# Router products issued among the row-tile transposes in three feed-forward stages

## The chip, the cores and the metric

The kernel runs on one core of a Trainium2 chip. The metric is the device time of one execution in microseconds (us); lower is better. The engines are named as in the profile: PE is TensorE's matmul side, PEld its weight loads, DVE is VectorE, ACT is ScalarE, POOL is GpSimd, SP is SyncE, which only starts DMAs here.

## The reference, cut to what matters

The program is a four-layer network over 2048 tokens (2 x 1024) of width 256. Each layer adds a gated cross-attention and then a gated mixture-of-experts feed-forward to `x`. The feed-forwards of layers 0, 1 and 3 choose experts per token from a linear router; what the change touches is that router's first step:

```python
# layer 0: x here is the layer-normalised input, 2048 x 256, Wr is 256 x 8
router_logits = x @ Wr
router_probs = softmax(router_logits, axis=-1)
expert_idx = argmax(router_probs, axis=-1)
...
# layer 1: Wg is 256 x 8, two experts per token
gating = softmax(X @ Wg + bg, axis=-1)
...
# layer 3: wg is 32 x 256, four experts per token out of four of eight groups
logits = xf @ wg.T
scores = softmax(logits, axis=-1)
```

Everything behind it (which expert, which row of the expert's buffer, the experts' own products, the sum back into `x`) depends on these logits. All arithmetic is float32.

## The kernel before, in words

Tokens lie in SBUF as 16 row tiles of 128 tokens (`TILES = 16`), each 256 wide, so a tile has two 128-column chunks (`DC = 2`). The kernel is written engine by engine: each stage is a block in which every engine has its own list of instructions in program order, and the engines meet through semaphores. No scheduler reorders anything; a stage ends in a barrier of all engines.

A feed-forward stage (`l0_ffn`, `l1_ffn`, `l3_ffn`) begins alike in all three layers. DVE computes the layer-norm statistics (`row_statistics`), then normalises tile after tile (`normalize_dve`, L115; in layer 3 the loop at L2830) and counts `staged` up. PE turns each normalised tile: two transposes per tile into one of four PSUM banks (`turn_pe`, L126; in layer 3 the same loop written out at L2730). ACT copies each turned tile from PSUM to `chip.xt` in SBUF (`turn_act`, L136) and counts `turned_read`; PE waits for that count before it reuses a bank. These two transposes of a tile are called T below.

When all 16 tiles have been turned, PE multiplies them by the router's weights (L604, L832, L2736): per tile two matmuls, one per chunk, with the turned tile as stationary operand and 8 columns of weights (32 in layer 3) as the moving one. These are called R. A float32 matmul runs as two passes, each with its own weight load, so R has two matmuls per tile in the program and four in the trace, 64 for the stage; T has two in both, 32 for the stage. One weight load with its matmul is called a pair: a stage has 96 of them.

The last R counts `routed`. DVE waits for it, then walks a chain of small operations (softmax, choice, ranks with two more matmuls by `rank_pe`, slots) up to `placed`. POOL waits for `placed` and scatters the rows to the experts' buffers in DRAM with indirect DMAs; SP waits for the scatters and loads the first expert's rows; PE waits for those. While all this goes on, SP's queue clears the buffers and loads the first experts' weights.

The lines of the transposes' loop and of R in layer 0 before:

```python
turn_pe(pe, chip, turn, p_hidden)
pe.wait_ge(loaded, 16)
for t in range(TILES):
    pe.wait_ge(turn.turned_read, t + 1)
    for c in range(DC):
        ins = pe.matmul(p_route[:, t * E:(t + 1) * E], chip.xt[:, c, t * P:(t + 1) * P], wr[:, c, :], ...)
ins.then_inc(routed, 1)
```

`turn_pe` is also called in the attentions of layers 1 and 3 and in the feed-forward of layer 2; those calls have no R with them in the changed kernel either.

Of the kernel before, what the change touches and what calls it, by code (L numbers as in the profile page):

```python
# [115 lines left out]
                          ALU.subtract, ALU.mult).then_inc(s.staged, 1)  # L116


def turn_pe(pe, chip, s, psum):

    for t in range(TILES):
        pe.wait_ge(s.staged, t + 1)
        if t >= TURN_BANKS:
            pe.wait_ge(s.turned_read, t + 1 - TURN_BANKS)
        for c in range(DC):
            ins = pe.transpose(psum[:, t % TURN_BANKS, c * P:(c + 1) * P], chip.xn[:, t, c * P:(c + 1) * P], chip.ident[:])  # L126
        ins.then_inc(s.turned, 1)


def turn_act(act, chip, s, psum, scale=None, bias=None):  # L130
# [374 lines left out]
def l0_ffn(nc, chip, I):  # L505
# [10 lines left out]
    with ExitStack() as stack:  # L516
# [78 lines left out]
        @block.tensor  # L595
        def _(pe):
            pe.wait_ge(b_loaded, 16)
            pe.transpose(p_y[:, 0:E * FC], b1_rows[:], chip.ident[0:E * FC, 0:E * FC]).then_inc(b1_turned, 1)
            turn_pe(pe, chip, turn, p_hidden)
            pe.wait_ge(loaded, 16)  # L600
            for t in range(TILES):
                pe.wait_ge(turn.turned_read, t + 1)
                for c in range(DC):
                    ins = pe.matmul(p_route[:, t * E:(t + 1) * E], chip.xt[:, c, t * P:(t + 1) * P], wr[:, c, :],  # L604
                                    start=c == 0, stop=c == DC - 1)
            ins.then_inc(routed, 1)
            pe.wait_ge(chose, 1)
            rank_pe(pe, chip, chosen[:], p_route[:, 128:256].rearrange("p (e t) -> p e t", e=E),
                    p_route[:, 256:384].rearrange("p (e t) -> p e t", e=E)).then_inc(ranked, 1)
            pe.wait_ge(placed, 1)  # L610
            pe.sem_inc(h_done, FC)
            pe.sem_inc(y_done, 1)

            def turn_rows(loads):
                pe.wait_ge(x_loaded, loads)
                for c in range(DC):
                    ins = pe.transpose(p_xt[:, c * P:(c + 1) * P], x_tile[:, c * P:(c + 1) * P], chip.ident[:])
                ins.then_inc(x_turned, 1)

            turn_rows(16)  # L620
            g = one_register(pe, "l0f_pe_g")
            with pe.Fori(0, E // 2) as i:
                for u in range(2):
                    pe.wait_ge(w_loaded[u], i * 32 + 32)
                    pe.sem_inc(passed, 1)
                    with tiles_of_expert(pe, tile_counts, i * 2 + u, g, MAX_TILES) as at:
                        pe.wait_ge(x_kept, at)
                        for f in range(FC):
                            for c in range(DC):
                                ins = pe.matmul(p_hidden[:, f // CB, (f % CB) * P:(f % CB + 1) * P], w1[:, u, c, f * P:(f + 1) * P], xt_tile[:, c * P:(c + 1) * P],  # L630
                                                start=c == 0, stop=c == DC - 1)
                            ins.then_inc(h_done, 1)
                        turn_rows(at * 16 + 16)
                        pe.wait_ge(y_kept, at)
                        for f in range(FC):
                            pe.wait_ge(h_kept, at * FC + (f + 1))
                            ins = pe.matmul(p_y[:, 0:D], hidden[:, f, :], w2[:, u, f, :], start=f == 0, stop=f == FC - 1)
                        ins.then_inc(y_done, 1)
# [80 lines left out]
def l1_ffn(nc, chip, I):  # L719
# [7 lines left out]
    with ExitStack() as stack:  # L727
# [95 lines left out]
        @block.tensor  # L823
        def _(pe):
            pe.wait_ge(b_loaded, 32)
            pe.transpose(p_y[:, 0:2 * E * FC], b13_rows[:], chip.ident[0:2 * E * FC, 0:2 * E * FC]).then_inc(b_turned, 1)
            turn_pe(pe, chip, turn, p_h)
            pe.wait_ge(loaded, 32)
            for t in range(TILES):
                pe.wait_ge(turn.turned_read, t + 1)  # L830
                for c in range(DC):
                    ins = pe.matmul(p_route[:, t * E:(t + 1) * E], chip.xt[:, c, t * P:(t + 1) * P], wg[:, c, :],  # L832
                                    start=c == 0, stop=c == DC - 1)
            ins.then_inc(routed, 1)
            pe.wait_ge(chose, 1)
            rank_pe(pe, chip, chosen[:], p_route[:, 128:256].rearrange("p (e t) -> p e t", e=E),
                    p_route[:, 256:384].rearrange("p (e t) -> p e t", e=E)).then_inc(ranked, 1)
            pe.wait_ge(placed, 1)
            pe.sem_inc(h_done, 4)
            pe.sem_inc(y_done, 1)  # L840

            def turn_rows(loads):
                pe.wait_ge(x_loaded, loads)
                for c in range(DC):
                    ins = pe.transpose(p_xt[:, c * P:(c + 1) * P], x_tile[:, c * P:(c + 1) * P], chip.ident[:])
                ins.then_inc(x_turned, 1)

            turn_rows(16)
            g = one_register(pe, "l1f_pe_g")
            with pe.Fori(0, E // 2) as i:  # L850
                for u in range(2):
                    pe.wait_ge(w_loaded[u], i * 48 + 48)
                    pe.sem_inc(passed, 1)
                    with tiles_of_expert(pe, tile_counts, i * 2 + u, g, MAX_TILES) as at:
                        pe.wait_ge(x_kept, at)
                        pe.wait_ge(h3_kept, at * 4)
                        pe.wait_ge(h13_kept, at * 4)
                        for half in range(2):
                            for bank, w in ((2 + half, w3), (half, w1)):
                                for f in (2 * half, 2 * half + 1):  # L860
                                    for c in range(DC):
                                        ins = pe.matmul(p_h[:, bank, (f % 2) * P:(f % 2 + 1) * P], w[:, u, c, f * P:(f + 1) * P],  # L862
                                                        xt_tile[:, c * P:(c + 1) * P], start=c == 0, stop=c == DC - 1)
                                ins.then_inc(h_done, 1)
                        turn_rows(at * 16 + 16)
                        pe.wait_ge(y_kept, at)
                        for f in range(FC):
                            pe.wait_ge(h_kept, at * 3 + max(f, 1))
                            ins = pe.matmul(p_y[:, 0:D], hidden[:, f, :], w2[:, u, f, :], start=f == 0, stop=f == FC - 1)
                        ins.then_inc(y_done, 1)  # L870

            pe.wait_ge(b2_loaded, 48)
            for t in range(TILES):
                s = t % 4
                if t >= 2:
                    pe.wait_ge(mixed_kept, t - 1)
                pe.wait_ge(mix_steps, 2 * t + 2)
                for c in range(DC):
                    ins = pe.transpose(p_h[:, t % 2, c * P:(c + 1) * P], mixed[:, s, c * P:(c + 1) * P], chip.ident[:])
                ins.then_inc(mixed_turned, 1)  # L880
                pe.wait_ge(mixed_kept, t + 1)
                if t >= 2:
                    pe.wait_ge(added, t - 1)
                for c in range(DC):
                    pe.matmul(p_h[:, 2 + t % 2, 0:D], mixed_t[:, s, c * P:(c + 1) * P], wf[:, c, :], start=c == 0, stop=False)
                pe.matmul(p_h[:, 2 + t % 2, 0:D], chip.ones[0:1, :], bf[:], start=False, stop=True).then_inc(out_done, 1)
# [1688 lines left out]
def l3_ffn(nc, chip, I, out):  # L2575
# [14 lines left out]
    with ExitStack() as stack:  # L2590
# [129 lines left out]
        def _(pe):  # L2720
# [1 line left out]
            for c in range(DC):  # L2722
                ins = pe.transpose(p_y[:, 0, c * E:(c + 1) * E], wg_rows[:, c * P:(c + 1) * P], chip.ident[0:E, 0:E])
            ins.then_inc(wg_turned, 1)
            for t in range(TILES):
                pe.wait_ge(turn.staged, t + 1)
                if t >= TURN_BANKS:
                    pe.wait_ge(turn.turned_read, t + 1 - TURN_BANKS)
                for c in range(DC):
                    ins = pe.transpose(p_h[:, t % TURN_BANKS, c * P:(c + 1) * P], x_ext[:, t, c * P:(c + 1) * P], chip.ident[:])  # L2730
                ins.then_inc(turn.turned, 1)
            pe.wait_ge(wg_kept, 1)
            for t in range(TILES):
                pe.wait_ge(turn.turned_read, t + 1)
                for c in range(DC):
                    ins = pe.matmul(p_y[:, 1, t * E:(t + 1) * E], chip.xt[:, c, t * P:(t + 1) * P], wg[:, c, :],  # L2736
                                    start=c == 0, stop=c == DC - 1)
            ins.then_inc(routed, 1)

# [222 lines left out]
```

## Time and profile before

| | us |
|---|---|
| median of 3 runs | 3436.51 |
| lowest and highest run | 3435.71, 3441.28 |
| span of the profiled execution (first to last instruction) | 3429.7 |
| busy in the span: PE, PEld, DVE, ACT, POOL | 2900.1, 2111.7, 1886.9, 1407.8, 608.0 |
| mean granted TensorE clock over the span | 0.902 |

The profiled execution is known by its span; it is 6.8 us shorter than the median of the runs, which are timed from outside. A time in the trace is counted from the span's start. The granted clock is given as a share of 2.4 GHz: 1.00 is 2.4 GHz, 0.50 is 1.2 GHz, and it has no level between; a value between belongs to a stretch in which it changed. A busy share over the whole span says little here, since the program is a row of stages with different limits: the stretches of the three feed-forward beginnings are near 106, 794 and 2973 us.

### The profile page before, as it was taken

The page shows a single profiled execution, that of the slowest core. Times are in us where ns is not written, and L with a number is a line of the kernel's source. Part 1 is how long each engine was busy: PE and PEld are TensorE (multiplying, and loading weights), DVE is VectorE, ACT ScalarE, POOL GpSimd, SP SyncE. Part 2 cuts the span into 40 slices and gives each one's busy share as a digit, 9 for nine tenths or more (in the row PEclk, how much of TensorE's full clock was granted, in tenths as well). Part 3 has the DMA queues.
Part 4 walks back from the last instruction along what each step waited for, and adds up shares of the span by engine and source line. Part 5 has one row for each costly group of instructions (what it writes and reads, how often), then busy time and mean ns, then how long its engine had stood idle before and what let it go on. Part 6 is the DMA issues. An engine that isn't in the chain of part 4 may idle for free. (4 is left out here: it accounts for less than half of the span.)

```text
span 3429.7 us, 46832 instructions
## 1 busy us (share of the span) xinstructions
PE 2900.1 (85%) x13932; PEld 2111.7 (62%) x13933; DVE 1886.9 (55%) x3558; ACT 1407.8 (41%) x2923; POOL 608.0 (18%) x571
## 2 busy tenths in 40 slices
PE   6495879972898798999789999999999998355997
PEld 5495545532786487999556666666666665233664
DVE  4312555403454336444478888888888886352332
ACT  1141544420221114444447777776777776100110
POOL 0202111113102120000201111111111111144554
PEclk7698889985998598999889999999999999577998
DMA  1443010005222101000010001000011000425775
GB/s 37 168 144 96 1 27 14 14 1 217 84 99 77 35 1 50 25 24 0 10 28 21 22 14 35 14 21 20 15 25 24 22 14 2 168 81 152 173 172 134
DMA packets 158692, 195.46 MB, mean 57 GB/s; under 512 B 39057, under 2 KB 129320, under 8 KB 154952
## 3 DMA queue, kind: packets, MB, share of 16 engines
q1 hardware_dynamic: 122072, 131.88, 12.8%
q0 software_dynamic: 22192, 40.13, 4.9%
q10 hardware_dynamic: 14304, 22.02, 1.9%
q8 instruction: 50, 0.82, 0.1%
q14 instruction: 74, 0.61, 0.1%
HBM read 105.38 MB, written 67.80 MB: 50 GB/s over the span
## 5 line engine op out<-in xcount | busy, mean ns | idle before, releaser
L1849 ACT ACTIVATE l3a_pt_hi<-l3a_banks 128x512 fp32r<-128x512 f32 (+2 forms) x640 | 382.0, 597 | 316.7 <-PE l3a_banks L1795 253.8
L1956 DVE TENSOR_TENSOR l3a_pt_lo<-l3a_pt,l3a_pt_hi 128x512 fp32r<-128x512 f32 (+2 forms) x640 | 460.3, 724 | 90.5 <-ACT l3a_pt L1850 85.9
L1850 ACT ACTIVATE l3a_pt<-l3a_banks 128x512 f32<-128x512 f32 (+2 forms) x640 | 378.0, 591 | 0.0
L1930 DVE TENSOR_REDUCE l3a_maxima<-l3a_banks 128x1 f32<-128x1178 f32 x256 | 351.4, 1376 | 2.4 <-PE l3a_banks L1746 1.1
L1795 PE MATMUL l3a_banks<-l3a_pt_hi,l3a_v 128*65 128x512 f32 (+2 forms) x640 | 286.3, 447 | 7.7 <-ACT l3a_out L1864 7.7
L1805 PE MATMUL l3a_banks<-l3a_q,l3a_k 128*128 128x512 f32 (+2 forms) x640 | 256.8, 401 | 7.2 <-ACT l3a_pt L1850 3.3
L1806 PE MATMUL l3a_banks<-l3a_q,l3a_k 72*128 72x512 f32 (+5 forms) x640 | 253.6, 396 | 0.0
L1795 PE MATMUL l3a_banks<-l3a_pt_hi,l3a_v_lo 128*65 128x512 f32 (+2 forms) x640 | 252.6, 395 | 0.0
L1795 PE MATMUL l3a_banks<-l3a_pt_lo,l3a_v 128*65 128x512 f32 (+2 forms) x640 | 252.4, 394 | 0.0
L1746 PE MATMUL l3a_banks<-l3a_k,l3a_q 128*128 128x512 f32 (+1 forms) x768 | 216.2, 392 | 15.4 <-DVE l3a_maxima L1930 14.3
L1746 PEld LDWEIGHTS l3a_banks<-l3a_k,l3a_q 128*128 128x128 f32 x768 | 141.8, 195 | 61.6 <-DVE l3a_maxima L1930 39.3
L2713 POOL DMA_INDIRECT l3f_sums<-l3f_y_rows,l3f_token_index x96 | 145.7, 1518 | 155.4 <-DVE l3f_row_weight L2905 130.7
L1984 POOL PARTITION_BROADCAST l3a_shared<-l3a_inverse x65 | 63.3, 975 | 618.2 <-issue 618.2
L1988 POOL TENSOR_TENSOR l3a_out_t<-l3a_out,l3a_shared 64x512 f32<-64x512 f32 x65 | 88.2, 1356 | 473.7 <-issue 473.7
L1805 PEld LDWEIGHTS l3a_banks<-l3a_q,l3a_k 128*128 128x128 f32 (+2 forms) x640 | 115.8, 181 | 78.1 <-ACT l3a_pt L1850 9.9
L1795 PE MATMUL l1a_banks<-l1a_pt,l1a_v 128*65 128x512 f32 (+2 forms) x320 | 153.3, 602 | 1.7 <-ACT l1a_out L1864 1.7
L1437 ACT ACTIVATE l2f_hidden_hi<-l2f_p_h,l2f_b_pair 128x512 fp32r<-128x512 f32 x128 | 89.2, 697 | 151.3 <-PE l2f_p_h L1390 140.1
L2821 ACT ACTIVATE l3f_silu<-l3f_p_h 128x320 f32<-128x320 f32 x64 | 28.0, 437 | 295.7 <-PE l3f_p_h L2783 295.7
L1489 DVE TENSOR_TENSOR l2f_hidden_lo<-l2f_hidden,l2f_hidden_hi 128x512 fp32r<-128x512 f32 x128 | 88.6, 692 | 107.6 <-ACT l2f_hidden L1438 107.6
L862 PE MATMUL l1f_p_h<-l1f_xt_tile,l1f_w 128*128 128x128 f32 x1184 | 141.5, 278 | 7.1 <-issue 6.1
L862 PEld LDWEIGHTS l1f_p_h<-l1f_xt_tile,l1f_w 128*128 128x128 f32 x1184 | 136.8, 194 | 14.9 <-issue 14.8
L2783 PE MATMUL l3f_p_h<-l3f_xt,l3f_w 128*128 128x320 f32 x512 | 144.5, 436 | 1.1 <-DVE l3f_xt L2895 1.1
(524 smaller groups left out, 6053.1 us busy)
## 6 DMA issues: line engine op xcount, KB each, us to landing
l3f_w<-in_L_ffn_w SPq DMA_DIRECT2D x96, 256.0 KB, 3.2
l0f_w<-in_L_ffn_W ACTq DMA_DIRECT2D x12, 1024.0 KB, 6.6
l3f_slots_x<-l3f_empty SPq DMA_DIRECT2D x10, 1168.0 KB, 14.3
l3f_x_rows<-l3f_slots_x SPq DMA_DIRECT2D x32, 292.0 KB, 3.9
l1f_w<-in_L_ffn_W ACTq DMA_DIRECT2D x18, 512.0 KB, 4.6
l2f_w<-in_L_ffn_w SPq DMA_DIRECT2D x16, 512.0 KB, 4.7
l3a_q<-l3a_q SPq DMA_DIRECT2D x64, 128.0 KB, 2.3
l3a_k<-l3a_k SPq DMA_DIRECT2D x64, 128.0 KB, 2.3
```

The lines of the kernel that those rows point to most:

```text
L862: ins = pe.matmul(p_h[:, bank, (f % 2) * P:(f % 2 + 1) * P], w[:, u, c, f * P:(f + 1) * P], xt_tile[:, c * P:(c + 1) * P], start=c == 0, s ...
L1437: act.activation(hidden_hi[:, n % 2, f, :], p_h[:, f, :], ACT.Gelu, bias=bias)
L1746: ins = pe.matmul(banks[:, c, 0:end - at], lhs, a.k1[:, u, h, at:end], start=True, stop=not masked)
L1795: ins = pe.matmul(a.o_bank[0:HEAD + 1, :], v[0:rows, u, c, h, :], pt[0:rows, slot, :], start=c == 0 and k == 0, stop=c == KEY_CHUNKS - 1 a ...
L1805: pe.matmul(a.st_bank[0:rows, n % 2, :], a.k1[:, u, h, row:row + rows], a.q1[:, u, h, queries], start=True, stop=False)
L1806: pe.matmul(a.st_bank[0:rows, n % 2, :], a.k2[second, u, h, row:row + rows], a.q2[second, u, h, queries], start=False, stop=True).then_inc ...
L1849: act.activation(a.pt_hi[0:rows, n % a.pt_slots, :], a.st_bank[0:rows, n % 2, :], ACT.Exp, bias=bias, scale=scale)
L1850: act.activation(a.pt[0:rows, n % 4, :], a.st_bank[0:rows, n % 2, :], ACT.Exp, bias=bias, scale=scale).then_inc(a.exped, 1)
L1930: dve.tensor_reduce(a.maxima[:, n:n + 1], banks.rearrange("p a b -> p (a b)")[:, 0:KEYS], AX.X, ALU.max).then_inc(a.maxed, 1)
L1956: dve.tensor_tensor(a.pt_lo[0:rows, slot, :], a.pt[0:rows, n % 4, :], a.pt_hi[0:rows, slot, :].bitcast(F32), ALU.subtract).then_inc(a.lo_m ...
L2713: pool.indirect_dma_start(sums, bass.IndirectOffsetOnAxis(token_index[0:n, u, j:j + 1], 0), y_rows[0:n, u, j, :], None, compute_op=ALU.add ...
L2783: ins = pe.matmul(p_h[:, k + f, 0:CAP], w[:, u, c, f * P:(f + 1) * P], xt[:, u, c, :], start=c == 0, stop=c == DC - 1)
```

## The change

In the three stages PE no longer does all T and then all R. `turn_pe` takes a `route` function and calls it for tile t - 2 right behind the transposes of tile t; the last two tiles' R follow behind the last transposes. Each R waits for ACT's copy of its own tile, as before. The waits for the router's weights (`loaded` in layers 0 and 1, `wg_kept` in layer 3) now stand ahead of the first transpose. Layer 3 calls `turn_pe` instead of its own copy of the loop. Nothing is added or taken away from the arithmetic, the buffers or the DMAs.

```diff
+ROUTE_LAG = 2
...
+def turn_pe(pe, chip, s, psum, source=None, route=None):
...
+    source = chip.xn if source is None else source
     for t in range(TILES):
         pe.wait_ge(s.staged, t + 1)
         if t >= TURN_BANKS:
             pe.wait_ge(s.turned_read, t + 1 - TURN_BANKS)
         for c in range(DC):
-            ins = pe.transpose(psum[:, t % TURN_BANKS, c * P:(c + 1) * P], chip.xn[:, t, c * P:(c + 1) * P], chip.ident[:])
+            ins = pe.transpose(psum[:, t % TURN_BANKS, c * P:(c + 1) * P], source[:, t, c * P:(c + 1) * P], chip.ident[:])
         ins.then_inc(s.turned, 1)
+        if route is not None and t >= ROUTE_LAG:
+            pe.wait_ge(s.turned_read, t - ROUTE_LAG + 1)
+            route(t - ROUTE_LAG)
+    if route is None:
+        return None
+    for t in range(TILES - ROUTE_LAG, TILES):
+        pe.wait_ge(s.turned_read, t + 1)
+        ins = route(t)
+    return ins
...
-            turn_pe(pe, chip, turn, p_hidden)
             pe.wait_ge(loaded, 16)
-            for t in range(TILES):
-                pe.wait_ge(turn.turned_read, t + 1)
+
+            def route(t):
                 for c in range(DC):
                     ins = pe.matmul(p_route[:, t * E:(t + 1) * E], chip.xt[:, c, t * P:(t + 1) * P], wr[:, c, :],
                                     start=c == 0, stop=c == DC - 1)
-            ins.then_inc(routed, 1)
+                return ins
+
+            turn_pe(pe, chip, turn, p_hidden, route=route).then_inc(routed, 1)
```

The edit of layer 1 reads the same with its own names; in layer 3 the loop of transposes goes and `turn_pe(pe, chip, turn, p_h, x_ext, route)` stands for it.

PE's list in the feed-forward of layer 0, from the bias transpose to the rank matmuls, before (`l0f_p_hidden<-chip_ident` is T, `l0f_p_route<-l0f_wr` is R, one row of the list stands for the program's matmuls, not for their passes):

```order
L598 MATMUL l0f_p_y<-chip_ident,l0f_b_rows 128x64
L126 MATMUL l0f_p_hidden<-chip_ident,chip_xn 128x128 x32
L604 MATMUL l0f_p_route<-l0f_wr,chip_xt 128x8 x32
L441 MATMUL l0f_p_route<-l0f_chosen,chip_before 128x128
L442 MATMUL l0f_p_route<-l0f_chosen,chip_ones 128x128
```

The beginning of the same list in the changed kernel:

```order
L612 MATMUL l0f_p_y<-chip_ident,l0f_b_rows 128x64
L131 MATMUL l0f_p_hidden<-chip_ident,chip_xn 128x128 x6
L617 MATMUL l0f_p_route<-l0f_wr,chip_xt 128x8 x2
L131 MATMUL l0f_p_hidden<-chip_ident,chip_xn 128x128 x2
L617 MATMUL l0f_p_route<-l0f_wr,chip_xt 128x8 x2
L131 MATMUL l0f_p_hidden<-chip_ident,chip_xn 128x128 x2
L617 MATMUL l0f_p_route<-l0f_wr,chip_xt 128x8 x2
```

The 32 transposes in a row have become six, and then two at a time with the two matmuls of an earlier tile behind them.

The end of the list in layer 3, changed (`l3f_p_h<-chip_ident` is T, `l3f_p_y<-l3f_wg` is R):

```order
L131 MATMUL l3f_p_h<-chip_ident,l3f_x_ext 128x128 x2
L2745 MATMUL l3f_p_y<-l3f_wg,chip_xt 128x32 x2
L131 MATMUL l3f_p_h<-chip_ident,l3f_x_ext 128x128 x2
L2745 MATMUL l3f_p_y<-l3f_wg,chip_xt 128x32 x6
L2773 MATMUL l3f_p_y<-l3f_chosen,chip_before 128x512
L2774 MATMUL l3f_p_y<-l3f_chosen,chip_ones 128x512
```

Behind the last transposes six matmuls of R are left, those of three tiles, where 32 stood before.

## Rows read from the trace of the kernel before

**Rows 1.** The page's first line.
```profile
span 3429.7 us, 46832 instructions
```
**Rows 2.** Waits: who waited for whom, us in total, times, longest.
```profile
POOL l0f_slots_x L582 <- DVEq L694: 31.0, 1, 31.0
PE l0f_p_xt L617 <- DMA l0f_x_tile<-l0f_slots_x: 28.0, 1, 28.0
...
POOL l1f_slots_x L809 <- DVEq L950: 36.1, 1, 36.1
...
POOL l3f_slots_x L2704 <- DVEq L2880: 8.9, 1, 8.9
```
**Rows 3.** Timeline, layer 0: start, us, engine, line, tiles, count, idle before it.
```profile
96.42 0.37 SPq L553 DMA_DIRECT2D l0f_wr<-in_L_ffn_Wr  x1
...
105.68 5.26 DVE L115 TENSOR_SCALAR chip_xn<-chip_x,chip_mean,chip_inv_std 128x256 f32<-128x256 f32 x16
...
106.15 6.06 PE L126 MATMUL l0f_p_hidden<-chip_ident,chip_xn 128*128 128x128 f32 x32 [6.87 <-DVE chip_xn L115]
...
106.88 5.89 ACT L136 COPY chip_xt<-l0f_p_hidden 128x256 f32<-128x256 f32 x16 [15.42 <-PE l0f_p_hidden L126]
...
112.05 8.65 PE L604 MATMUL l0f_p_route<-l0f_wr,chip_xt 128*128 128x8 f32 x64
...
120.74 0.29 DVE L678 TENSOR_REDUCE l0f_best<-l0f_p_route 128x16 f32<-128x128 f32 x1 [9.66 <-PE l0f_p_route L604]
```
**Rows 4.** Timeline, layers 1 and 3, the same places.
```profile
794.02 5.45 PE L126 MATMUL l1f_p_h<-chip_ident,chip_xn 128*128 128x128 f32 x32 [6.02 <-DVE chip_xn L115]
...
809.07 0.29 DVE L930 TENSOR_TENSOR l1f_logits<-l1f_p_route,l1f_bg 128x128 f32<-128x128 f32 x1 [10.12 <-PE l1f_p_route L832]
...
2972.88 0.22 DVE L2828 COPY l3f_wg<-l3f_p_y 128x64 f32<-128x64 f32 x1
...
2973.48 6.04 PE L2730 MATMUL l3f_p_h<-chip_ident,l3f_x_ext 128*128 128x128 f32 x32 [6.81 <-DVE l3f_x_ext L2830]
...
2988.20 0.69 DVE L2835 TENSOR_REDUCE l3f_best<-l3f_p_y 128x16 f32<-128x512 f32 x1 [9.91 <-PE l3f_p_y L2736]
```
**Rows 5.** Stretches: from:to, length, PE busy (count), granted clock, DMA share, GB/s.
```profile
106.15:110.71 4.56, 4.56 (x22) 0.50 1.01 408
110.71:112.05 1.34, 1.34 (x13) 1.00 1.02 422
112.05:117.54 5.49, 5.49 (x52) 1.00 0.99 337
117.54:120.70 3.16, 3.16 (x16) 0.50 1.08 374
794.02:796.79 2.77, 2.77 (x13) 0.50 1.01 417
...
803.62:809.03 5.41, 5.41 (x26) 0.50 1.00 409
2973.48:2977.91 4.43, 4.43 (x21) 0.50 1.01 422
...
2984.74:2988.16 3.42, 3.42 (x17) 0.50 1.01 420
```
**Rows 6.** One line's instructions in short stretches: count, ns min/median/max, first and last start.
```profile
L126 PE MATMUL l0f_p_hidden<-chip_ident,chip_xn x17: 421/421/421, 106.6 to 110.0; 128*128 128x128 f32 x17
...
L604 PE MATMUL l0f_p_route<-l0f_wr,chip_xt x39: 256/256/256, 112.8 to 117.0; 128*128 128x8 f32 x39
...
L604 PE MATMUL l0f_p_route<-l0f_wr,chip_xt x13: 361/361/362, 117.8 to 120.3; 128*128 128x8 f32 x13
...
L2736 PE MATMUL l3f_p_y<-l3f_wg,chip_xt x15: 401/401/402, 2984.8 to 2987.8; 128*128 128x32 f32 x15
```
**Rows 7.** Layer 3's attention, its 32 transposes by the same helper: line's starts, stretch.
```profile
L126 PE MATMUL l3a_banks<-chip_ident,chip_xn x32: 417/421/474, 1699.7 to 1709.3; 128*128 128x128 f32 x32
...
1699.70:1709.35 9.65, 9.24 (x32) 0.50 0.00 0
```

More of the change, by code:

```diff
@@ L116, in normalize_dve @@
                           ALU.subtract, ALU.mult).then_inc(s.staged, 1)
-def turn_pe(pe, chip, s, psum):
+ROUTE_LAG = 2
+def turn_pe(pe, chip, s, psum, source=None, route=None):
+    source = chip.xn if source is None else source
     for t in range(TILES):
@@ L826, in _, with route @@
             pe.transpose(p_y[:, 0:2 * E * FC], b13_rows[:], chip.ident[0:2 * E * FC, 0:2 * E * FC]).then_inc(b_turned, 1)
-            turn_pe(pe, chip, turn, p_h)
             pe.wait_ge(loaded, 32)
-            for t in range(TILES):
-                pe.wait_ge(turn.turned_read, t + 1)
+            def route(t):
                 for c in range(DC):
@@ L833, in _ @@
                                     start=c == 0, stop=c == DC - 1)
-            ins.then_inc(routed, 1)
+                return ins
+            turn_pe(pe, chip, turn, p_h, route=route).then_inc(routed, 1)
             pe.wait_ge(chose, 1)
@@ L2724, in _, with route @@
             ins.then_inc(wg_turned, 1)
[L2725 to L2731, printed above, removed]
             pe.wait_ge(wg_kept, 1)
-            for t in range(TILES):
-                pe.wait_ge(turn.turned_read, t + 1)
+            def route(t):
                 for c in range(DC):
@@ L2737, in _ @@
                                     start=c == 0, stop=c == DC - 1)
-            ins.then_inc(routed, 1)
+                return ins
+            turn_pe(pe, chip, turn, p_h, x_ext, route).then_inc(routed, 1)
             def shared_block(b):
```

## The prediction

> **What bounds the kernel now.** I first looked at where the three touched stretches stand in the chain of work, then at what PE does in them. The waits say that they are on the path in all three layers: POOL's scatter waits for DVE's routing chain for 31.0, 36.1 and 8.9 us, and PE's first expert waits 28.0 us for the scattered rows [rows 2]. At the head of that chain DVE waits for the last R: 9.66, 10.12 and 9.91 us of idle time stand before its first routing step [rows 3, 4]. So a microsecond more or less between the first transpose and that DVE step goes to the end of the kernel almost whole. I call that distance the stage's length. Before, it is 120.74 - 106.15 = 14.59 us in layer 0, 809.07 - 794.02 = 15.05 us in layer 1 and 2988.20 - 2973.48 = 14.72 us in layer 3 [rows 3, 4].
>
> Next, who is slow in these 14 to 15 us? PE. Cut where its granted clock changes, every stretch is busy from end to end: 4.56 of 4.56, 1.34 of 1.34, 5.49 of 5.49, 3.16 of 3.16 us [rows 5]. DVE normalises 16 tiles in 5.26 us, 0.33 us each, and ACT copies 16 in 5.89 us [rows 3], while PE at the low clock needs 2 x 0.213 = 0.427 us for a tile's two transposes (price below). There is no gap among the transposes into which R could slip. **Interleaving can therefore save nothing by filling PE's idle time; it only changes in which order PE does the same 96 pairs.** What is left to decide is at which clock it does them.
>
> The prices of a pair come from the starts of neighbouring matmuls [rows 6]. T at granted clock 0.50 (1.2 GHz): 17 starts from 106.6 to 110.0, 3.4 / 16 = 0.213 us. R at 0.50: 13 starts from 117.8 to 120.3, 2.5 / 12 = 0.21 us; layer 3's R with 32 columns, 15 starts in 3.0 us, the same 0.21. R at 1.00 (2.4 GHz): 39 starts from 112.8 to 117.0, 4.2 / 38 = 0.111 us. So T and R cost the same, 0.213 us at the low clock and 0.111 at the full one, whatever number of columns R moves. I use 0.2133 and 0.112 below, within what these roundings leave.
>
> Now the clock [rows 5]. In layer 0 it stands at 0.50 for the first 4.56 us of transposes, is 1.00 from 110.71 to 117.54, and falls to 0.50 for the last 3.16 us, in which 16 matmuls of R take what about 28 would take at 1.00. It rose while PE did nothing but transposes, and it fell after 5.49 us in which PE did nothing but R, without a pause. Layers 1 and 3 show the same: up after 2.77 and 4.43 us of transposes, down for the last 5.41 and 3.42 us of R. A dense row of transposes is what earned the clock in each of these stages, and R did not hold it, though PE counts as busy throughout.
>
> **The change part by part.** It takes away that dense row. After the first six transposes PE repeats four pairs of R and two of T: at 0.2133 us a pair, two transposes every 6 x 0.2133 = 1.28 us, 1.6 per us. In layer 0 before they came at 22 in 4.56 us, 4.8 per us [rows 5]. Between these the trace has one more case, the attention of layer 3: 32 transposes by the same helper in 9.65 us, 3.3 per us, and the clock stayed 0.50 to the end [rows 7]. The new stream has half that density of transposes, and R between them, which failed to hold the clock where it ran alone. I take it that **the clock stays at 0.50 through the whole stage**.
>
> Then a stage is 96 pairs at the low price: 95 x 0.2133 = 20.26 us from the first start to the last, plus the last matmul's 0.361 us (0.401 in layer 3) [rows 6] and 0.04 us until DVE starts: 20.67 us, 20.71 in layer 3. Against before:
>
> - layer 0: 20.67 - 14.59 = +6.1 us
> - layer 1: 20.67 - 15.05 = +5.6 us
> - layer 3: 20.71 - 14.72 = +6.0 us
>
> Sum +17.7 us. Seen another way, each stage loses some 6.83 us at full clock, 61 pairs at 0.112, which cost 0.101 more each: 61 x 0.101 = 6.2 us, less the little that transposes at full clock had lost to waiting for ACT.
>
> The other edits. The wait for the router's weights, moved ahead of the transposes, costs nothing: layer 0's `wr` was issued at 96.42, nearly 10 us before the first transpose [rows 3]; layer 3's copy of `wg` starts at 2972.88 and ends 0.4 us before the first transpose at 2973.48 [rows 4], and DVE does it ahead of the normalising that PE waits for anyway. If the weights came late, the price would be that lateness, once per stage; behind PE's wait then stand all transposes and ACT's copies. The new wait of R for ACT's copy two tiles back costs nothing either: from the first transpose's start at 106.15 to the first copy's start is 0.73 us, and a copy takes 5.89 / 16 = 0.37 us [rows 3], 1.10 us in all; between a tile's transposes and its R lie at least the six first transposes, 1.28 us, and later 14 pairs, 2.99 us. Queued behind that wait would be the next transposes, and behind them ACT. The four PSUM banks are now never the limit, as R's wait has already seen a later copy. No DMA, POOL or SP instruction moves; DVE and ACT have their old lists. Later work moves 6 us against its weight loads, which only come earlier relative to it. A later clock change can fall a little differently: I allow 3 us to either side over the rest of the kernel, about half the spread of the three runs (3435.71 to 3441.28).
>
> The sum stands against the profiled execution's span of 3429.7 us [rows 1], which would become 3447.4. The median of the runs is 6.8 us longer than the span; with it, 3436.5 + 17.7 = **3454.2 us**, with 3451 to 3458 as this case's own range.
>
> **The rivals.** *A: the mixed stream gets the full clock when the transposes did, and keeps it.* This is the case not slower. For it speaks that PE is just as busy as before from end to end, and that transposes recur in the stream, where before 5.49 us of R had none. Against it speak both facts above: the clock fell under uninterrupted R, and did not rise under 3.3 transposes per us [rows 5, 7]. The Trainium skill's page "TensorE: Matmul & The Clock Gate", section "Why this matters for your kernels", has it that an engine kept continuously busy with matmuls gets past the low clock; by that rule this rival would be the outcome. The trace agrees for transposes and disagrees for R, which was continuous and lost the clock. Price: 21.4 pairs in the first 4.56 us, then 74.6 at 0.112 = 8.4 us, and 0.3 at the end: 13.2 us in layer 0, -1.4; likewise 2.77 + 83 x 0.112 + 0.3 = 12.4 us in layer 1, -2.7, and 4.43 + 75.2 x 0.112 + 0.3 = 13.1 us in layer 3, -1.6. Sum -5.7 us, 3430.8. It decides where 1.6 transposes per us with R between them suffice. If the clock rises but falls again as before, there is nothing to win, 3436. Even the best of this is no gain over 0.2%, 6.9 us, which is about what a measurement of this kernel can tell from no change.
>
> *B: only layer 3 gets the clock*, since its R moves 32 columns where the others move 8. Against it: its R alone lost the clock like the others. Price: 6.1 + 5.6 - 1.6 = +10.1 us, 3446.6.
>
> *C: the lag of two tiles is too short and PE stands still before each R.* It decides if a tile's way through ACT takes over 2.99 us, where the rows give 1.10. If each of the 14 R among the transposes waited for one copy of 0.37 us, a stage would grow by 5.2 us more: 17.7 + 15.6 = +33.3, 3470. That the change does something else than it says is ruled out by PE's list in the changed kernel.
>
> **How the numbers follow.** The forecast has 0.78, A 0.12, B 0.06, C 0.04. Forecast, B and C are slower by over 0.2%: 0.88. Of A I give 0.09 to no difference and 0.03 to a gain over 0.2%, for the case that a later stage also gains some clock. The range reaches from B with its error down to 3444, and up to 3462, between the forecast's upper end and C; A and C stay outside, 0.16.
>
> **What would show it.** In the changed trace each of the three stages should show granted clock 0.50 from its first transpose to its last R, 361 ns as the duration of R's matmuls in layers 0 and 1 where 256 stood for those at full clock, and DVE's wait for R grown from about 10 us to 16. The mean granted clock should fall from 0.902 to about 0.897: 3 x 6.83 us less at full clock. Layer 2's feed-forward, which has the same helper and an unchanged order, should keep its length. The prediction is wrong if a stretch among the mixed pairs shows 1.00, if PE has gaps before R, or if the stage grows by 6 us and the scatter behind it does not start later.

## The result and the profile after

The changed kernel takes 3446.2 us, median of 12 runs (3440.5 to 3458.4), the kernel before 3437.65 us in the 12 runs beside it (3429.5 to 3443.1). The ratio is 1.0028 with a 95% interval of 1.0015 to 1.0041: the change makes the kernel slower by 9.6 us (0.28%), 5 to 14 us; the two medians differ by 8.6 us.

The first rows to read are the three stretches from the first transpose to DVE's first routing step, one line each for layers 0, 1 and 3 (from:to, length, PE busy and count, granted clock, DMA share, GB/s). Before:

```profile
106.15:120.74 14.59, 14.55 (x96) 0.73 1.02 376
794.02:809.07 15.05, 15.01 (x96) 0.73 1.01 415
2973.48:2988.20 14.72, 14.68 (x96) 0.73 1.01 423
```

After:

```profile
94.90:114.10 19.20, 19.13 (x96) 0.50 1.03 374
789.60:808.76 19.16, 19.12 (x96) 0.50 1.00 392
2981.60:3000.88 19.28, 19.17 (x96) 0.50 1.01 423
```

The same 96 matmuls, PE counted as busy from end to end in both; what differs is the granted clock. (A matmul's record is longer than the step to the next one, 0.36 us against 0.21 at the low clock, so a short wait can hide in a full busy time; where it matters below, the steps between starts are read instead.) The spell at 1.00 that each stage had [rows 5] is gone from all three, and they are 19.2 us long (19.16, 19.16 and 19.20 from the first transpose's own start; the windows above begin up to 0.08 us earlier). Against the stages of before that is +4.6, +4.1 and +4.5 us, 13.2 in the sum.

One line's instructions in layer 0, and who waited for it (us, times); R is L617 now:

```profile
L617 PE MATMUL l0f_p_route<-l0f_wr,chip_xt x64: 221/361/361, 96.2 to 113.7; 128*128 128x8 f32 x64
...
who waited for it (us, times):
  DVE l0f_best L693: 14.3, 1
```

R's median matmul is 361 ns, the duration that [rows 6] show at 0.50, and the stretch above has 0.50 throughout: nothing of R ran at 1.00 any more. (The 221 ns belong to the first R behind each pair of transposes, also at 0.50; more on it below.) DVE waits 14.3 us for it where it had waited 9.66 [rows 3].

The waits further down the chain, in layers 0 and 1:

```profile
POOL l0f_slots_x L596 <- DVEq L709: 35.6, 1, 35.6
...
POOL l1f_slots_x L824 <- DVEq L966: 40.3, 1, 40.3
```

They stood at 31.0 and 36.1 us [rows 2]: the scatter begins 4.6 and 4.2 us later relative to POOL's own start, as much as the stages have grown. In layer 3 POOL's wait for `placed` stayed at 8.9 us, because POOL has an earlier wait in the same chain, and that one grew, from 54.7 to 59.3 us. The first scatter of layer 3, before and after (timeline):

```profile
3034.88 1.23 POOL L2704 DMA_INDIRECT l3f_slots_x<-l3f_x_ext,l3f_scatter_index  x1 [8.87 <-DVEq L2880]
3047.58 1.23 POOL L2720 DMA_INDIRECT l3f_slots_x<-l3f_x_ext,l3f_scatter_index  x1 [8.88 <-DVEq L2891]
```

That is 46.7 us behind DVE's first routing step in both (2988.20 and 3000.88). In layers 0 and 1 the scatter begins 9.4 and 13.4 us behind that step in both kernels, and PE's first expert 33.2 and 57.4 us behind it (57.1 in layer 3), within 0.1 us. So up to the first expert none of the delay is made up in any of the three layers.

### The profile page after: what moved, and what is told of

It is laid out like the page before. It is cut to its first block and busy times, and to the rows that moved or that the text cites. A ratio compares the mean times of both kernels' runs of the same rounds, so it can differ in the third digit from the quotient of the medians.

```text
span 3446.4 us, 46832 instructions
## 1 busy us (share of the span) xinstructions
PE 2915.7 (85%) x13932; PEld 2126.6 (62%) x13933; DVE 1881.5 (55%) x3558; ACT 1411.1 (41%) x2923; POOL 611.5 (18%) x571
## 5 line engine op out<-in xcount | busy, mean ns | idle before, releaser
L878 PEld LDWEIGHTS l1f_p_h<-l1f_xt_tile,l1f_w 128*128 128x128 f32 x1184 | 137.6, 195 | 14.9 <-issue 14.7
```

## The experiments

Eight more kernels ran, and both kernels of the case once more, all on one chip. The theory under test is the prediction's: the stage is longer because the mixed stream does not get the full clock. Its rival is that mixing costs by itself, through waits for ACT's copies or through the changes between transposes (T) and router matmuls (R).

**Putting a denser row back.** In the first two only the lag differs from the changed kernel.

```diff
-ROUTE_LAG = 2
+ROUTE_LAG = 12
```

> The changed kernel with a lag of 12 tiles in place of 2: 26 transposes stand in a row before the first R; then three tiles mixed, then the rest of R. Clock theory (the stage is longer because no dense row of transposes earns the full clock): the clock rises to 1.00 among the dense transposes as it did before the change, for 6.8 us or longer, and a stage from first transpose to DVE's first routing step is 13.5 to 15.5 us, as before (14.6 to 15.1). Rival, the mixing itself costs (waits for ACT, switches between transposes and R): the three mixed tiles of 14 keep their share of the 4.4 us that the change cost, about 1 us more than before, 15.6 to 16 us, at whatever clock.

The three stages (same columns as above):

```profile
96.14:113.29 17.15, 17.11 (x96) 0.60 1.02 378
789.69:806.83 17.14, 17.10 (x96) 0.60 1.01 408
2975.99:2990.31 14.32, 14.28 (x96) 0.74 1.01 423
```

The clock came back in all three, but for 3.4 us in two of them and 6.8 us in the third (the mean clock's excess over 0.50, times twice the length): 17.1, 17.1 and 14.3 us. My expectation of 13.5 to 15.5 us missed two of three, because I took the length of the spell from a single execution. The rival's 15.6 to 16 us, the same in each stage, missed all three. Three stages with the same list differ by 2.8 us, so what sets the length is not the list alone; with a mean clock of 0.60 they are 17.1 us, with 0.74 14.3 us.

With a lag of 8:

> The same with a lag of 8 tiles: 18 transposes in a row (3.8 us at the low clock), then seven mixed tiles, then R. Clock theory: stage by stage one of two lengths, nothing between them in proportion to the mixing: where the dense row earns the clock 13 to 15 us, with a stretch at 1.00; where it does not, 19 to 20 us, all at 0.50. Rival, the mixing costs: half of the 4.4 us in every stage, 17 us, without regard to the clock.

```profile
104.03:123.84 19.81, 19.77 (x96) 0.50 1.02 372
801.42:815.09 13.67, 13.63 (x96) 0.75 1.01 415
2980.79:2992.64 11.85, 11.81 (x96) 0.88 1.01 424
```

Nearly one list of instructions, apart from layer 3's 32 columns, and three lengths between 11.85 and 19.81 us, in the order of the clock. That is the clear case against the rival: half the mixing does not cost half, it costs what the clock makes of it. My own expectation allowed two lengths, 13 to 15 or 19 to 20 us; the 11.85 us lie outside, as there the clock, once up after 2.9 us, stayed up to the end, through seven mixed tiles and the R behind them. The single times of the two kernels, 3434.9 and 3436.9 us, say little beside a kernel before that runs from 3430 to 3446 us in the 23 runs of this set.

**Giving the clock before the stage begins.** PE is idle while DVE computes the norms, so it was given 28 transposes of the identity into a PSUM tile that nothing uses yet.

```diff
+WARM = 28
...
+def warm_pe(pe, chip, out):
...
+    for _ in range(WARM):
+        pe.transpose(out, chip.ident[:], chip.ident[:])
...
+            warm_pe(pe, chip, p_xt[:, 0:P])
             turn_pe(pe, chip, turn, p_hidden, route=route).then_inc(routed, 1)
```

With the order of before (lag 16):

> The order of before (lag 16: all transposes, then all R), and PE does 28 transposes of the identity into an unused PSUM tile just before each of the three stages, while DVE still computes the norms and PE would be idle. Clock theory: the first real transpose finds 1.00; DVE's 0.33 us per tile then sets the pace of the transposes (5.3 us), R begins at 0.112 us a pair and falls to 0.50 somewhere in its 64: a stage of 12.5 to 14 us, 1 to 2 us less than before, 3 to 6 us in the sum, about 3433 where before gives 3437. Rival, the clock does not matter for the length: 14.6 to 15.1 us as before.

Its stages were 15.0, 14.9 and 15.6 us, and the ratio to the kernel before 0.9987 (0.9976 to 0.9998). So the first transpose did find 1.00, but the stages gained nothing in this profile (45.5 us in the sum; the two profiles of the kernel before have 44.4 and 46.9), against what I expected. Layer 0, cut at the fall:

```profile
99.44:108.75 9.31, 9.31 (x71) 1.00 1.00 367
108.75:114.45 5.70, 5.66 (x28) 0.50 1.05 386
```

The full clock was spent on the transposes, which DVE paces at 0.33 us a tile when PE is fast, and was lost again in R: 28 of its matmuls ran at the low price. Whether the small gain in the total comes from these stages is left open.

With the changed order (lag 2):

> The changed order (lag 2) with the same 28 transposes of the identity ahead of each stage. Clock theory: the stage begins at 1.00 and stays there for 3.4 us at least; where the mixed stream holds the clock it takes 10.5 to 11.5 us, where it loses it 13 to 16 us, in either case several us under the 19.2 us of the changed kernel; the sum over the stages falls by 10 to 25 us against the changed kernel. Rival, the mixing itself costs (waits for ACT, switches): a stage stays at 19 us or near it, since PE would wait as before.

Layer 0 up to the fall and behind it, then layer 1 whole, then layer 3 up to the fall and behind it:

```profile
105.36:107.91 2.55, 2.55 (x22) 1.00 1.00 392
107.91:122.82 14.91, 14.87 (x76) 0.50 1.02 373
800.38:810.86 10.48, 10.44 (x96) 1.00 1.02 417
2979.97:2981.93 1.96, 1.96 (x16) 1.00 1.03 428
2981.93:2997.95 16.02, 15.98 (x82) 0.50 1.01 426
```

In layer 1 the clock happened to hold, and the 96 matmuls of the mixed stream went through in 10.48 us, 0.109 us each, with every wait for ACT and every change between T and R in it. So neither waits nor changes cost anything of note. In layers 0 and 3 the stream began at 1.00 and lost it after 2.55 and 1.96 us, where I had expected at least 3.4, and the stages took 17.5 and 18.0 us: one stage came out at the low end of my expectation, and the other two were 1.5 to 2 us longer than it allowed. The total has a ratio of 0.9983 (0.9969 to 0.9998). Why layer 1 held the clock and the others did not is not settled.

**Making R hold the clock.** The cleanest test leaves the number of matmuls, the weight loads and the order alone and changes only what R moves: 128 columns, the router's 8 (or 32) repeated by a stride of zero. (In layer 3 the last three tiles move 96, 64 and 32.) The surplus columns are overwritten later or never read.

```diff
-                    ins = pe.matmul(p_route[:, t * E:(t + 1) * E], chip.xt[:, c, t * P:(t + 1) * P], wr[:, c, :],
-                                    start=c == 0, stop=c == DC - 1)
+                    ins = pe.matmul(p_route[:, t * E:t * E + P].rearrange("p (r e) -> p r e", e=E), chip.xt[:, c, t * P:(t + 1) * P],
+                                    wr[:, c, :].unsqueeze(1).to_broadcast([P, P // E, E]), start=c == 0, stop=c == DC - 1)
```

With the changed order, without the warm-up:

> The changed order (lag 2), but each matmul of R moves 128 columns in place of 8 (layer 3: 32): the router's 8 columns repeated by a stride of zero, the surplus results overwritten by the next tile's. A pair at the full clock should cost 0.109 to 0.112 us as before, since a pair of a transpose, which also moves 128 columns, costs that. Clock theory: the mixed stream now earns the clock as the row of transposes did, after 2.8 to 5 us, and keeps it to the end: a stage of 12 to 13.5 us in all three layers, against 19.2 in the changed kernel; total 3431 to 3435 against 3439.9 of before. Rival, mixing itself costs or the clock follows the share of time in which PE is busy (which does not change): 19 to 20.5 us at 0.50, total as the changed kernel.

Each stage up to the rise of the clock and from there to its end, layers 0, 1 and 3:

```profile
104.50:110.12 5.62, 5.62 (x27) 0.50 0.99 399
110.12:118.07 7.95, 7.91 (x71) 1.00 1.02 350
793.42:796.19 2.77, 2.77 (x13) 0.50 1.00 414
796.19:805.63 9.44, 9.40 (x85) 1.00 1.01 413
2975.79:2980.73 4.94, 4.94 (x24) 0.50 1.01 423
2980.73:2988.95 8.22, 8.18 (x74) 1.00 1.01 421
```

The order is the changed kernel's to the instruction, PE is busy from end to end as there, and R does sixteen times (layer 3: up to four times) the arithmetic; yet the clock rises within 2.8 to 5.6 us, does not fall again, and the stages take 13.6, 12.2 and 13.2 us instead of 19.2. The total is 3430.2 us, ratio to the kernel before 0.9970 (0.9955 to 0.9984).

With the order of before and the same R:

> The order of before (all transposes, then all R) with R moving 128 columns. Clock theory: the clock rises as before and does not fall during R: a stage of 12 to 13.5 us, the same as with the mixed order, since PE is busy throughout in both. Rival, the order decides: clearly different from the mixed order with the same R. If the fall of the clock before had another cause than the few columns R moves, it falls again after 6.8 us and the stage takes 14.5 to 15 us.

```profile
106.97:120.13 13.16, 13.12 (x96) 0.84 1.00 375
794.98:808.66 13.68, 13.64 (x96) 0.79 1.01 416
2977.60:2990.67 13.07, 13.03 (x96) 0.84 1.02 427
```

13.1 to 13.7 us, as with the mixed order: at nearly equal clocks the order hardly matters where PE is the limit. And the fall of the clock in the kernel before was due to R's few columns: with 128 of them it did not fall in any of the three stages, where it fell in all six of the two profiles with few. The kernel's time is a single run, 3437.6 us, and says nothing beside the spread.

Both together, warm-up and wide R, with the changed order:

> The changed order, R moving 128 columns, and 28 transposes of the identity ahead of each stage. Clock theory: 1.00 from the first transpose to the last R in all three stages, 96 pairs at 0.109 to 0.112: 10.4 to 11 us each, 12 to 13 us less than before in the sum; total about 3427, and under both kernels. Rival, the clock at the start is luck and the stream loses it as it did twice with the narrow R: stages of 17 to 18 us.

and with the order of before:

> The same with the order of before. Clock theory: 1.00 throughout, but now DVE's 0.33 us a tile paces the transposes (5.3 us) and PE idles among them; then 64 pairs of R at 0.112, 7.2 us: 12.4 to 12.8 us a stage. So at a full clock the mixed order should be worth 2 us a stage, 6 us in all, which it could not show at the low clock. Rival, mixing is worth nothing at any clock: the same length as the mixed order within 0.3 us.

Stages of the mixed order, then of the order of before, each for layers 0, 1 and 3:

```profile
106.86:118.05 11.19, 11.15 (x96) 1.00 1.00 376
795.02:806.21 11.19, 11.15 (x96) 1.00 1.02 417
2970.01:2981.09 11.08, 11.04 (x96) 1.00 1.01 422
```

```profile
102.33:114.80 12.47, 12.43 (x96) 1.00 1.01 376
789.95:802.42 12.47, 12.43 (x96) 1.00 1.02 415
2970.07:2982.37 12.30, 12.26 (x96) 1.00 1.00 419
```

1.00 throughout in all six. Here the mixed order is worth 1.2 to 1.3 us a stage (I had expected 2), because at the full clock PE waits for DVE among the transposes when they stand alone, and R can fill that. The busy time does not show this wait; the starts do. Layer 1 with the order of before:

```profile
789.95 5.29 PE L138 MATMUL l1f_p_h<-chip_ident,chip_xn 128*128 128x128 f32 x32 [1.13 <-DVE chip_xn L115]
795.08 7.31 PE L854 MATMUL l1f_p_route<-l1f_wg,chip_xt 128*128 128x128 f32 x64
```

The 32 transposes take 5.13 us up to the first R, 0.16 us each, which is DVE's 0.33 us a tile. The mixed kernel takes 3423.8 us, ratio to the kernel before 0.9961 (0.9943 to 0.9979), 13 us less than before and better than both kernels; the other has 3431.2 us and 0.9980 (0.9968 to 0.9992). A stage is a little over my 10.4 to 11 us: 0.117 us a matmul, where the one stage at full clock with the narrow R had 0.109. The two transposes of one mixed tile and of the next, narrow and then wide, both in layer 1:

```profile
806.70 0.41 PE L138 MATMUL l1f_p_h<-chip_ident,chip_xn 128*128 128x128 f32 x2
807.31 0.41 PE L138 MATMUL l1f_p_h<-chip_ident,chip_xn 128*128 128x128 f32 x2
801.13 0.38 PE L138 MATMUL l1f_p_h<-chip_ident,chip_xn 128*128 128x128 f32 x2
801.79 0.38 PE L138 MATMUL l1f_p_h<-chip_ident,chip_xn 128*128 128x128 f32 x2
```

A tile takes 0.61 us with the narrow R and 0.66 with the wide one, which is six pairs at 0.11; 14 mixed tiles make this 0.7 us, the whole difference of the two stages. A row of wide R by itself (layer 1 above) costs (7.31 - 0.27) / 63 = 0.112 us a matmul, the narrow one 0.111 [rows 6].

**How much is chance.** Both kernels of the case were profiled once more.

> The kernel before, profiled once more, to see how much a stage's length differs between executions. Clock theory: each stage has one spell at 1.00 that begins among the transposes and ends in R; where it is 6.8 us long the stage is 13.5 to 15.2 us, where it is shorter correspondingly longer, about 0.9 us for each us at 1.00. Rival, the stage's length is fixed by its instructions: 14.6, 15.0 and 14.7 us again within 0.2.

Layer 0 in three parts, then layers 1 and 3 whole:

```profile
103.82:109.53 5.71, 5.71 (x27) 0.50 1.00 406
109.53:112.94 3.41, 3.41 (x33) 1.00 1.02 326
112.94:121.26 8.32, 8.28 (x40) 0.50 1.03 381
795.75:810.65 14.90, 14.86 (x96) 0.73 1.02 418
2978.55:2993.09 14.54, 14.50 (x96) 0.73 1.01 425
```

Layer 0's spell at 1.00 was 3.41 us this time and the stage 17.44 us, where the first profile had 6.83 and 14.59. The sum of the three stages is 46.9 us here and 44.4 there.

> The changed kernel, profiled once more. Clock theory: no spell at 1.00 in the three stages, and so no spread: 19.1 to 19.3 us each. Rival, the missing spell was chance: at least one of the stages has one and is shorter by a us or more.

```profile
105.51:124.67 19.16, 19.13 (x96) 0.50 1.02 374
799.92:819.09 19.17, 19.13 (x96) 0.50 1.00 393
2984.22:3003.42 19.20, 19.16 (x96) 0.50 1.01 425
```

The changed kernel repeats to 0.02 us: no spell, no spread. Of the 24 stages profiled with the narrow R, in all orders, 21 follow one rule: no time at 1.00 gives 19.2 to 19.8 us, 2 to 3.4 us give 17.1 to 18.0, 6.8 us give 13.7 to 15.05, 9 us give 11.9 (lag 8, layer 3), 10.5 us give 10.5. Only the three of the warmed order of before stand outside (8.5 to 9.5 us at 1.00, 14.9 to 15.6 us), since its transposes spend the full clock waiting for DVE. What sets the length of a spell, and whether one comes at a lag of 8, stays open. The single times of these two kernels are 3435.7 and 3449.5 us.

## Why the prediction was right, and which terms were off

**What bounds the stage: right.** PE is busy for 19.13 of 19.20 us after the change; there was no idle time to fill, and at the low clock the mixed order saves only the 1.5 us a stage that are worked out below.

**The path to the end: right as far as the first expert.** DVE's wait for R grew by what the stage grew in layer 0 (9.66 to 14.3 us), and scatter and first expert kept their distance from DVE's step in all three layers. Behind that, single executions differ by several us in stretches that the change does not touch: from DVE's step in layer 1 to the first transpose of layer 3 it is 2164 and 2168 us in the two profiles of before, 2173 and 2165 in the two of the changed kernel.

**The clock: right, and shown by more than the profile of the change.** The prediction took from [rows 5, 7] that the dense row of transposes earned the clock and that R did not hold it. The changed kernel has 0.50 in six of six stages. With R widened to 128 columns and nothing else changed, the clock came and stayed, with the transposes as thinly spread as in the changed kernel. So a dense row of transposes was one way to the clock and not the only one: going from 8 to 128 columns in R alone brought it back. Rival A, the mixed stream gets the full clock, is therefore out for the changed kernel; with R at 128 columns a mixed stream kept it in six of six stages. The rule weighed there, from the Trainium skill's page "TensorE: Matmul & The Clock Gate", section "Why this matters for your kernels", that keeping the engine continuously busy gets it past the low clock, does not fit here: PE was busy for 19.1 us on end at 0.50, and with the same order and a wider R it was at 1.00 after 2.8 to 5.6 us. The measurement decides: being busy was not enough here, it mattered what the matmuls moved. R's failure to hold the clock is no strict rule either: the narrow mixed stream kept it for 10.48 us in layer 1 of the warmed kernel and lost it in layers 0 and 3. Rival B, layer 3 alone gets it with its 32 columns: out, 19.20 us at 0.50. Rival C, PE stands still before R: out by the steps in the timeline below, where a mixed tile takes less than its six pairs, and by the 10.48 us of layer 1 in the warmed kernel.

**The size: two terms off.** Predicted +17.7 us, 3454.2; measured +9.6 (5 to 14), 3446.2. That is below the forecast's own 3451 to 3458, and inside the stated range only because this was stretched down to rival B's price; the total lies on that price, 3446.6, by chance. Only the clock of each stage tells the two apart. The first wrong term is "95 x 0.2133": the stage was to be 20.67 us and is 19.16. The mixed stream is cheaper than its pairs one by one. PE's timeline of the changed kernel:

```profile
102.83 0.67 PE L131 MATMUL l0f_p_hidden<-chip_ident,chip_xn 128*128 128x128 f32 x2
103.29 0.86 PE L617 MATMUL l0f_p_route<-l0f_wr,chip_xt 128*128 128x8 f32 x4
104.00 0.67 PE L131 MATMUL l0f_p_hidden<-chip_ident,chip_xn 128*128 128x128 f32 x2
```

A tile's six pairs go from 102.83 to 104.00, 1.17 us, where 6 x 0.2133 gives 1.28: two transposes take 0.46 us to the first R, and four R take 0.71 us to the next transpose, 0.14 less than four pairs: the second R starts 0.07 us behind the first, not 0.21. With 14 mixed tiles that is 1.5 us a stage, the whole difference; three stages, 4.5 us. I had priced rows of equal pairs and none of the changes between kinds.

The second is the base. The lengths 14.59, 15.05 and 14.72 came from one execution in which each of the three spells at 1.00 was 6.83 us long. The second profile has one of 3.41 us and a sum 2.5 us longer; set against that execution the change costs 57.5 - 46.9 = 10.6 us, against the first 13.2, and the runs' interval holds both. How much of the 3.6 us between 13.2 and 9.6 is the base is not shown, since single executions differ by more than that outside the stages. The profiled execution was also a quick one by chance: the changed kernel's profiled run took 3448.25 us with a span of 3446.4, 1.9 us more, so by estimate a span of 3429.7 belongs to a run of about 3431.6 us, and most of the 6.8 us between span and median is not the timing from outside but chance. I gave the lengths no range of their own.

**What was said of the rest** held: the mean granted clock is 0.896 where 0.897 was expected (the changed kernel's other runs have 0.892 to 0.901, so agreement to a thousandth is luck), and the unchanged feed-forward of layer 2 has 7.48 us from its first transpose to the next DVE step, before 7.36.

## What to carry to other kernels

A float32 matmul with its own weight load cost 0.213 us at the low clock here whether it moved 8, 32 or 128 columns, and a stretch of narrow ones can sit at 1.2 GHz however busy the engine looks: read the granted clock of the stretch before planning to fill or reorder it. Where a dense row of transposes earns the clock, thinning it out with narrow matmuls can cost more than any overlap brings; make the narrow ones wide first (here by repeating columns, at 0.117 instead of 0.109 us a matmul in the mixed stream), then overlap. When a stage's length depends on a clock that comes and goes, one profile gives one sample of it: take two, and give the base a range.

## What was not expected of the hardware

- In a row of its own at full clock R takes 0.112 us a matmul with 128 columns and 0.111 with 8: sixteen times the columns at nearly the same price. The mixed stream takes 0.117 us a matmul with the wide R, 0.109 with the narrow one.
- Changes between transposes and narrow R make the stream faster than either alone: 1.17 us for six pairs instead of 1.28 at the low clock, 0.61 where the wide R takes 0.66 at the full one.
- The same order of instructions took 11.85 (with 32 columns), 13.67 and 19.81 us (both with 8) in three layers of one execution (lag 8).
- The runs of one kernel spread over 3424 to 3448 us (25 runs of the kernel before). In the two profiles of the changed kernel the first transpose of layer 0 comes at 94.9 and at 105.5 us, ten microseconds apart in the stage ahead, which the change does not touch; yet the two runs took 3448.25 and 3449.54 us, so other stretches made up for it.
